# Layer normalisation scaled on another engine, and the first batch placed from SBUF to SBUF, in an attention and mixture-of-experts kernel

## The reference

```python
def _layernorm(x, axis=-1, eps=1e-05):
    m = jnp.mean(x, axis=axis, keepdims=True)
    v = jnp.var(x, axis=axis, keepdims=True)
    return (x - m) / jnp.sqrt(v + eps)

# attention: 16 heads of 16 channels, 256 queries, 512 keys (256 projected, 256 memory rows)
q = x1 @ Wq + bq;  k = concat(x2 @ Wk + bk, memory);  v = concat(x2 @ Wv + bv, memory)
out = softmax(q @ k.T * 0.25) @ v;  x = x + out @ Wp + bp
# experts: 8 of 256 -> 1024 -> 256, all of them applied to all tokens
g = x2 @ w_gate;  u = x2 @ w_up;  h = silu(g) * u;  expert_out = h @ w_down
cw = softmax(x2 @ w_router) * softmax(x2 @ w_gating / 0.1), normalised over the experts
x = x + sum_e cw[e] * expert_out[e]
```

## Time and profile before

| | |
|---|---|
| median of 3 runs | 2712.37 us (2711.29 to 2715.34) |
| profiled execution | 2711.55 us |
| its span, first to last instruction | 2709.8 us |
| PE busy | 2660.4 us (98%) |
| DVE busy | 2007.7 us (74%) |
| POOL busy | 1651.8 us (61%) |
| ACT busy | 1526.0 us (56%) |
| mean granted clock of TensorE | 0.991 of full speed |
| chain that ended last, by engine | PE 94%, DVE 4%, issue 1%, DMA 1% |

### The profile page before, as it was taken

The page is one execution under the profiler, slowest core; times in us unless marked ns, Lnnn a source line. Parts: engine busy times, 40 slices in busy tenths (PEclk is TensorE's granted clock), DMA queues, the critical chain, the costliest instruction groups (busy, mean ns, idle before and its releaser), DMA issues.

```text
span 2709.8 us, 46807 instructions
## 1 busy us (share of the span) xinstructions
PE 2660.4 (98%) x15969; PEld 2184.3 (81%) x15969; DVE 2007.7 (74%) x3303; ACT 1526.0 (56%) x2887; POOL 1651.8 (61%) x1837
## 2 busy tenths in 40 slices
PE   6899999999999999999999999999999999999998
PEld 5578888888888888888888888888888888888887
DVE  6987777777778777777777777777787777655554
ACT  4655555555555555555555555555555555544443
POOL 4766666666656666566666566666566666655554
PEclk8899999999999999999999999999999999999999
DMA  6344434444333443433434433444333442333332
GB/s 166 101 112 122 127 100 118 132 120 123 115 118 115 120 126 115 127 109 112 131 115 131 120 116 108 125 122 131 113 105 114 126 122 88 97 107 113 108 102 82
DMA packets 298427, 315.44 MB, mean 116 GB/s; under 512 B 22096, under 2 KB 269264, under 8 KB 298192
## 3 DMA queue, kind: packets, MB, share of 16 engines
q1 hardware_dynamic: 298192, 312.45, 39.0%
HBM read 278.15 MB, written 33.69 MB: 115 GB/s over the span
## 4 chain that ended last, share of the span: by engine, by line
PE 94%; DVE 4%; issue 1%; DMA 1%; POOL 0%; ACT 0%; SPq 0%; POOLq 0%; DVEq 0%; ACTq 0%
PE ps_s L706 26%; PE ps_t L706 26%; PE ps_o L740 25%; PE ps_s L803 4%; PE ps_t L813 4%; PE ps_a L782 2%; PE ps_a L784 2%; PE ps_m L586 1%; PE ps_m L615 1%; DVE negmax L1187 1%; PE ps_m L604 1%; DVE Pt_lo L1059 1%; PE ps_m L659 0%; DMA d_k<-kT_lo 0%; PE ps_m L677 0%
## 5 line engine op out<-in xcount | busy, mean ns | idle before, releaser
L969 DVE SCALAR_TENSOR_TENSOR hf<-hf,ps_s 128x512 f32<-128x512 f32 x512 | 350.2, 684 | 326.7 <-ACT hf L827 324.8
L833 ACT ACTIVATE h_hi<-ps_t 128x512 fp32r<-128x512 f32 x512 | 306.1, 598 | 440.2 <-DVE ps_t L976 440.2
L1221 POOL TENSOR_TENSOR wg_lo<-stage_w,wg_hi 128x512 fp32r<-128x512 f32 x256 | 330.9, 1292 | 339.5 <-ACT wg_hi L840 337.9
L827 ACT ACTIVATE hf<-ps_s 128x512 f32<-128x512 f32 x512 | 306.4, 598 | 410.5 <-PE ps_s L706 410.5
L981 DVE TENSOR_TENSOR h_lo<-ps_t,h_hi 128x512 fp32r<-128x512 f32 x512 | 353.0, 689 | 211.9 <-ACT h_hi L833 205.6
L740 PE MATMUL ps_o<-h_lo,wd_hi 128*128 128x512 f32 x1024 | 400.1, 391 | 0.0
L740 PE MATMUL ps_o<-h_hi,wd_hi 128*128 128x512 f32 x1024 | 398.5, 389 | 0.9 <-DVE h_lo L981 0.9
L740 PE MATMUL ps_o<-h_hi,wd_lo 128*128 128x512 f32 x1024 | 398.4, 389 | 0.0
L976 DVE TENSOR_TENSOR ps_t<-hf,ps_t 128x512 f32<-128x512 f32 x512 | 356.4, 696 | 52.9 <-PE ps_t L706 6.2
L1221 POOL TENSOR_TENSOR wd_lo<-stage_w,wd_hi 128x512 fp32r<-128x512 f32 x256 | 330.8, 1292 | 93.0 <-ACT wd_hi L840 93.0
L947 ACT ACTIVATE Pt<-ps_t 128x512 f32<-128x512 f32 x512 | 305.8, 598 | 142.1 <-PE ps_t L813 134.1
(11 more groups left out here) (208 smaller groups left out, 4734.3 us busy)
## 6 DMA issues: line engine op xcount, KB each, us to landing
stage_w<-in_L_ffn_w_gate_dram SPq DMA_DIRECT2D x256, 256.0 KB, 2.8
stage_w<-in_L_ffn_w_up_dram SPq DMA_DIRECT2D x256, 256.0 KB, 3.1
stage_w<-in_L_ffn_w_down_dram SPq DMA_DIRECT2D x256, 256.0 KB, 2.8
KTs<-d_k SPq DMA_DIRECT2D x96, 256.0 KB, 4.9
cwb<-d_cw SPq DMA_DIRECT2D x64, 256.0 KB, 3.6
QTs<-d_q SPq DMA_DIRECT2D x192, 64.0 KB, 2.7
X<-in_x_dram SPq DMA_DIRECT2D x32, 256.0 KB, 4.5
d_k<-kT_hi SPq DMA_DIRECT2D x16, 512.0 KB, 4.1
```

The source lines that it names most:

```text
L827: act.activation(hf[:], ps_g[:], ACT.Tanh, scale=0.5).then_inc(tanh_done, 1)
L833: act.activation(h_hi[f % FC][:], ps_u[:], ACT.Copy).then_inc(hh_done, 1)
L969: dve.scalar_tensor_tensor(out=hf[:], in0=hf[:], scalar=1.0, in1=ps_g[:], op0=ALU.add, op1=ALU.mult).then_inc(gate_done, 1)
L1221: pool.tensor_tensor(lo[:], raw_weights(n), hi[:].bitcast(F32), ALU.subtract).then_inc(wl_done, 1)
```

## The change

1. **Statistics.** One `bn_aggr` for each of the two token tiles gives mean and variance, and two `tensor_scalar` of 128x2 add epsilon and negate the mean. They are ready one step earlier than before.
2. **Applying them.** GpSimd multiplies the negated mean by the scale into `shift` (one more instruction of 128x2). ScalarE computes scale * x + shift, at step 13 (`X1`) and step 28 (`X`, formerly 29 on VectorE).
3. **First batch.** `place_first` at step 10 of turn -1 copies each pair from `kT` and `qT` directly to `KTs` and `QTs`, 9 transfers for each of 8 pairs (3 of 64 KB, 6 of 16 KB), 72 in a row on SP. Batch 0 is not stored to DRAM and not read back. PE waits pair by pair; whoever overwrites `kT` or `qT` for batch 1 waits for all 72.
4. **First loads.** The three `stage_w` loads move to steps 20 to 22 of turn 0. `key_rows` has 3 rows instead of 32 (48 KB), the GpSimd memset of all of it is gone, and the key product reads 99 partitions.
5. **First q.** "q" of turn -1 gets its own PSUM bank, `ps_t[1]`.

```diff
@@ norm_stats
-                    dve.tensor_tensor(m[:, :, 2:4], stt[:, :, 1:3], stt[:, :, 4:6], ALU.add).then_inc(mv_c.sem, 1)
-                    dve.tensor_tensor(m[:, :, 1], stt[:, :, 1], stt[:, :, 4], ALU.subtract).then_inc(mv_c.sem, 1)
+                    for t in range(QT):
+                        dve.bn_aggr(m[:, t, 0:2], stt[:, t, :]).then_inc(mv_c.sem, 1)
                 if step == at + 2:
-                    turn.wait(dve, mv_c, d, 2)
-                    dve.tensor_scalar(m[:, :, 0], m[:, :, 2], 0.5, None, ALU.mult).then_inc(mv_c.sem, 1)
-                    dve.tensor_scalar(m[:, :, 4], m[:, :, 3], 1.0 / D, LN_EPS, ALU.mult, ALU.add).then_inc(mv_c.sem, 1)
-                    dve.scalar_tensor_tensor(out=m[:, :, 5], in0=m[:, :, 1], scalar=0.25, in1=m[:, :, 1],
-                                             op0=ALU.mult, op1=ALU.mult).then_inc(mv_c.sem, 1)
-                if step == at + 3:
-                    turn.wait(dve, mv_c, d, 5)
-                    dve.tensor_tensor(v[:], m[:, :, 4], m[:, :, 5], ALU.add).then_inc(ve_c.sem, 1)
+                    turn.wait(dve, mv_c, d, QT)
+                    dve.tensor_scalar(v[:], m[:, :, 1], LN_EPS, None, ALU.add).then_inc(ve_c.sem, 1)
+                    dve.tensor_scalar(m[:, :, 2], m[:, :, 0], -1.0, None, ALU.mult).then_inc(ve_c.sem, 1)
@@ GpSimd, step 26 (and the same at step 12 for X1)
                         pool.tensor_tensor(rstd[:], ve[:], neg_half[:], ALU.pow).then_inc(rstd_done.sem, 1)
+                        turn.wait(pool, rstd_done, 2, 1)
+                        pool.tensor_tensor(shift[:], mv[:, :, 2], rstd[:], ALU.mult).then_inc(shift_done.sem, 1)
@@ ScalarE (VectorE's normalise, called at steps 13 and 29, is gone)
+            def normalise(src, r, s, dst, done):
+                for t in range(QT):
+                    act.activation(dst[:, t, :], src[:, t, :], ACT.Identity, bias=s[:, t:t + 1],
+                                   scale=r[:, t:t + 1]).then_inc(done.sem, 1)
@@ SP
+            def place_first():
+                eng.wait_ge(k_l.sem, 2)
+                eng.wait_ge(m_l.sem, 1)
+                for pair in range(PAIRS):
+                    m, at = pair // GP, pair % GP * ROWS
+                    for slot, part in enumerate((kT_hi, kT_lo, kT_hi)):
+                        eng.dma_start(KTs[slot * ROWS:(slot + 1) * ROWS, pair, :].bitcast(F32),
+                                      part[at:at + ROWS, m, :].bitcast(F32)).then_inc(first_in[pair], 16)
+                    if pair == 0:
+                        eng.wait_ge(q_l.sem, 2)
+                        eng.wait_ge(const_ready, CONSTS)
+                    for slot, part in enumerate((qT_hi, qT_hi, qT_lo)):
+                        for h in range(2):
+                            to, row = slot * ROWS + h * HD, at + h * HD
+                            eng.dma_start(QTs[to:to + HD, pair, h, :].bitcast(F32),
+                                          part[row:row + HD, m, :].bitcast(F32)).then_inc(first_in[pair], 16)
@@ SP, the order of the steps
-                    if turn.has(1) and step == (10 if first else 14):
-                        store_keys(turn, 1)
...
+                    if turn.b == -1 and step == 10:
+                        place_first()
+                    if turn.b == 0 and step >= 20 and step - 20 < 3:
+                        load_weights(step - 20, 0)
@@ TensorE
+                        if turn.b + d == 0:
+                            if i % 4 == 0:
+                                pe.wait_ge(first_in[i // 4], 16 * 9)
...
-                        pe.matmul(key_bank(j)[:], KTs[:, pair, kc * P:(kc + 1) * P],
-                                  QTs[:, pair].rearrange("p h n -> p (h n)"),
+                        pe.matmul(key_bank(j)[:], KTs[0:USED, pair, kc * P:(kc + 1) * P],
+                                  QTs[0:USED, pair].rearrange("p h n -> p (h n)"),
@@ bank
-            return ps_m[:] if one else ps_o[:, 1, :]
+            return ps_t[1][:] if one is None else ps_m[:] if one else ps_o[:, 1, :]
```

More of the change, by code:

```diff
@@ L53, in bass_xattn_moe_ffn_kernel @@
     TOP = 3 * ROWS
+    USED = TOP + 3
     GP = PAIRS // 2
@@ L224, in bass_xattn_moe_ffn_kernel @@
         v_ps = Count("v_ps", 1); v_done = Count("v_done", 1)
+        first_in = [sem(f"first_in{p}") for p in range(PAIRS)]
         k_in = [Count(f"k_in{g}", 16 * 3) for g in range(2)]
@@ L245, in bass_xattn_moe_ffn_kernel, with wait_stored @@
         cwT_ps = Count("cwT_ps", 1); cwT_done = Count("cwT_done", 1)
-        CONSTS = 7
+        CONSTS = 6
         LAST = (START + FSTEPS) // STEPS
+        def wait_stored(eng, turn, count):
+            if turn.b == 0:
+                for arrived in first_in:
+                    eng.wait_ge(arrived, 16 * 9)
+            else:
+                turn.wait(eng, count, -1, 32)
         class Turn:
@@ L808, in body @@
                         pair, kc = i // KC, i % KC
+                        if turn.b == 0 and i == 0:
+                            pe.wait_ge(rows_in, 16)
                         if kc == 0:
@@ L881, in body @@
                         split_high(n)
+                    if step == 13 and turn.has(-1):
+                        turn.wait(act, shift2_done, -1, 1)
+                        turn.wait(act, x2T_ps, -2, 1)
+                        normalise(X1, rstd2, shift2, X2, x2_done)
+                    if step == 28 and turn.has(2):
+                        turn.wait(act, shift_done, 2, 1)
+                        turn.wait(act, xT_ps, 1, 1)
+                        normalise(X, rstd, shift, XN, xn_done)
                     for o, at, d in v_at(turn):
@@ L922, in body @@
                         turn.wait(act, full, 1, 1)
-                        turn.wait(act, used, 0, 32)
+                        wait_stored(act, turn, used)
                         for m in range(DC):
@@ L1060, in low_part @@
                                       ALU.subtract).then_inc(lo_dve.sem, 1)
-            def normalise(turn, d, src, m, r, dst, done):
-                for t in range(QT):
-                    dve.tensor_scalar(dst[:, t, :], src[:, t, :], m[:, t, 0:1], r[:, t:t + 1],
-                                      ALU.subtract, ALU.mult).then_inc(done.sem, 1)
             def body(turn):
@@ L1162, in body @@
                                           ALU.add).then_inc(x1_done.sem, 1)
-                    if step == 13 and turn.has(-1):
-                        turn.wait(dve, rstd2_done, -1, 1)
-                        turn.wait(dve, x2T_ps, -2, 1)
-                        normalise(turn, -1, X1, mv2, rstd2, X2, x2_done)
                     if name == "lg":
@@ L1177, in body @@
                                           ALU.subtract).then_inc(ldif_done.sem, 1)
-                    if step == 29 and turn.has(2):
-                        turn.wait(dve, rstd_done, 2, 1)
-                        turn.wait(dve, xT_ps, 1, 1)
-                        normalise(turn, 2, X, mv, rstd, XN, xn_done)
                     d, i = item_at(step, AHEAD)
@@ L1204, in _ @@
             pool.memset(zeros[:], 0.0).then_inc(const_ready, 1)
-            pool.memset(key_rows[:], 0.0).then_inc(rows_clear, 1)
             pool.memset(QTs[:].bitcast(F32), 0.0).then_inc(const_ready, 1)
```

85 lines of the change are left out of this document (44 added, 41 removed).

## The result

| | before | after |
|---|---|---|
| median | 2711.14 us (6 runs) | 2731.14 us (6 runs, 2728.82 to 2731.73) |
| ratio after / before, 95% interval | | 1.0070 (1.0057 to 1.0083) |
| profiled execution, its span | 2711.55, 2709.8 us | 2728.82, 2726.8 us |

The account below looks back on a forecast made before the run. PE was taken to bound the joint stage and VectorE the attention stage, with the opening ahead. From 2712.4 us, 3.2 us for the opening and 4.3 us for the normalisations gave -7.5 us: 2704.9 us, 8-in-10 range 2697 to 2712 us.

Parts of the forecast that it names:

- What bounds the kernel: Joint stage: PE always busy, so no gain there; attention stage: VectorE bound; the end moves as the experts' start does.
- The opening, up to the first score: Batch 0's first placing: SP issues at 14.5 us, first score at 21.1 us, 10.5 us sooner; 3.2 us finally kept.
- 72 issues ... 0.46 us each ... ends at 47.7 us: SP's queue in the opening: all placing transfers issue ahead of turn 0's work, bounds 0.43 to 0.51 us each.
- what is late next: Turn 0, step 12: VF load behind the 72 issues stalls PE's "m" 7 us, leaving 3.4 of 10.5 us.
- The normalisations: Four layer normalisations before the experts: net 6.5 us off VectorE, two thirds, 4.3 us, reaching the end; bounds 1 to 7.
- The stronger form with GpSimd's share given back: Attention stage: VectorE and GpSimd both regain time lost to their shared port lock, making the 4.3 us about 6.
- Slow copies: Rival, 8%: SBUF-to-SBUF data take 47 us, last pair lands at 62 us, VF behind it; about 2716 us.
- Fast placing: Rival, 12%: small transfers issue at 0.35 us, VF is not late, opening keeps 10 us; 2698 us.
- The gain stays in the opening: Rival, 29%: issues cost 0.51 us or VectorE's relief becomes waits for ScalarE; one part lost, 2707 to 2712 us.
- Edits at no cost: 99-partition key product, late stage_w loads and ScalarE's 0.84 us in the joint stage were claimed to cost nothing.

Follow-up runs that it names:

- own_tiles: Changed kernel with batch 0's keys and queries in tiles free until turn 1, the 72 transfers kept; 2726.37 us, ratio 1.0045.
- own_tiles_vf: own_tiles with the VF load issued ahead of the last 18 of the 72 transfers; 2719.18 us, ratio 1.0018.
- pair0_direct: Kernel before with parts 1, 2, 4 and 5, first of eight pairs copied SBUF to SBUF, seven by DRAM; 2705.49 us, ratio 0.9970.
- dram_source: Changed kernel with batch 0 stored to DRAM first and the same 72 transfers reading it there; 2724.19 us, one run.
- place_only: Changed kernel with the layer normalisations of the kernel before, parts 3, 4 and 5 left; 2732.82 us, ratio 1.0072.
- stats_only: Kernel before with bn_aggr and one small addition for the statistics, VectorE still applying mean and scale; 2710.82 us, ratio 0.9988.
- loads_only: Kernel before with parts 4 and 5 alone, batch 0 still by DRAM; 2711.94 us, ratio 0.9996.
- pair0_warm3: pair0_direct with three extra identity transposes on PE ahead of each small job of turns 0 and 1; ratio 0.9975.

## Why the prediction was wrong

Starts of steps on PE (the key product, from the timelines, us) beside what each kernel ends with. The steps and the spans are of one profiled execution each, the last row is of all runs:

| | before | after | own_tiles | own_tiles_vf | pair0_direct |
|---|---|---|---|---|---|
| turn 0, step 0 | 39.7 | 34.5 | 34.0 | 34.1 | 33.2 |
| turn 0, step 6 | 48.5 | 65.9 | 44.1 | 42.6 | 43.4 |
| turn 0, step 12 | 55.5 | 73.6 | 68.2 | 54.5 | 50.8 |
| turn 0, step 24 | 71.3 | 90.0 | 85.2 | 78.7 | 66.4 |
| turn 2, step 14 | 157.2 | 174.6 | 170.5 | 163.0 | 151.1 |
| span of that execution | 2709.8 | 2726.8 | 2724.7 | 2715.2 | 2705.8 |
| end, by the ratio | | +19.0 | +12.2 | +4.9 | -8.1 |

**What bounds the kernel.** Right. The joint stage gave nothing for VectorE's 64 us, and the end moved by about as much as the steps just ahead of the experts: step 14 of turn 2 is 17.4 us late in the changed kernel and its span 17.0 us longer.

**The opening, up to the first score.** The chain to SP's first issue was right within 0.1 us. The first score came at 22.53 us, 1.4 us later than forecast. The nine issues of the first pair ended at 21.28 us instead of 18.8. The six of `QTs` took 0.9 us more, and they began 1.6 us late: the third issue of the burst alone took 1.80 us, 1.2 us more than its neighbours (why is open), and the rest is the dearer issue. PE then began 1.25 us later, where 2.3 us had been taken. Step 0 of turn 0, which needs the third pair, started at 34.5 us instead of 29.4 us, because the pairs come every 5.7 us.

**The step that failed first: "72 issues ... 0.46 us each ... ends at 47.7 us".** The price came from placings whose source is DRAM, with bounds of 0.43 and 0.51 us from the same rows. For a copy from SBUF to SBUF it is 0.633 us, outside both; dram_source shows that the source makes the difference. 72 x (0.633 - 0.46) = 12.5 us, and the burst ended 13.7 us later than forecast; most of the rest is the one issue of 1.80 us. The rows were of another kind, and no upper bound was drawn for that. The prediction read the only SBUF-to-SBUF transfer in the trace as a rate of data and not for its issue, which took 0.75 us; 72 of those would be 54 us, past every case that it considered.

**The step that was left out: "what is late next".** It looked along SP's queue alone and found `VF` at step 12, which own_tiles confirms as the second wait. The first is at step 4: whoever overwrites `kT` waits for all 72. The change's own list said so, and the sum had no term for it. This omission decides even at the forecast's price: burst ended at 47.7 us, plus the 1.35 us measured from last issue to ScalarE, is 49.05 us, against 45.70 us in the kernel before. The 3.2 us gain of the opening becomes a loss of 3.4 us, and with 4.3 us for the normalisations the whole comes to about no change. The dearer issue then makes it 17.1 us late. dram_source confirms this reading near its own price: "k" 11.0 us late, the end 10.5 us late.

**From 17.1 to 19 us.** The profiled execution of the changed kernel is the fastest of its six. Its span is 17.0 us longer than that of the kernel before, as much as "k" is late; the other five are 1.7 to 2.9 us slower, and for those there is no trace. The changed kernel is also as slow as place_only (1.0070 and 1.0072), so the 3 us of the normalisations do not show in it. The intervals, each about 3.5 us to a side, leave this open.

**The normalisations.** 4.3 us forecast, 3.0 us measured, within the interval. `bn_aggr` took 0.156 us (0.1 taken), the first `tensor_scalar` 0.227 us instead of 0.63, ScalarE's instruction 0.59 us instead of 0.42. The size came out, but the argument for it, that VectorE is relieved by 10 us and so the end by two thirds of the net, is not borne out: stats_only leaves VectorE its two large instructions and gains as much. What ScalarE adds (two of 0.59 us for each normalisation, and 2.7 and 3.0 us of waiting for `shift` at the two `X1`) is a price on an engine between PE and VectorE. The stronger form with GpSimd's share given back, 6 us, lies outside the interval.

**The rivals.** *Slow copies* was the side on which it fell, at 8%, and by the wrong resource. It decided from 0.57 us per transfer on, and 0.633 us is past that. But it spoke of the time of the data, and it reached the loss by way of `VF`: in the changed kernel PE started "m" at 72.93 us without a wait for `VF`, since "k" had made everything later. In the DMA view of the changed kernel, 14 to 62 us, 16 engines are busy for a fifth and each transfer lands in 2 us:

```profile
DMA packets 2658, 2.37 MB, mean 49 GB/s; under 512 B 1136, under 2 KB 1888, under 8 KB 2656
...
q1 hardware_dynamic: 2656, 2.35, 19.9%
...
KTs<-kT_hi SPq DMA_DIRECT2D x16, 64.0 KB, 2.0
...
QTs<-qT_hi SPq DMA_DIRECT2D x32, 16.0 KB, 1.8
```

The engines had room; the queue that issues was full. The Trainium skill, "DMA: Bandwidth & Descriptors", section "Bandwidth", has it that transfers under 64 KB are dominated by descriptors. This trace is no test of that: its 49 GB/s follow from the time between two issues on SP. The same page of the Trainium skill, section "Anatomy of one DMA — SWDGE (gpsimd) path", speaks of another path, and calls the cost of generating descriptors small and variable. What part of an issue on SP that is, no run here shows; the whole issue was 0.45 or 0.63 us for every transfer, times 72. *Fast placing* asked for 0.35 us an issue: no run shows it. *The gain stays in the opening* describes loads_only, not the change.

**Edits at no cost.** The 99 partitions: right, nothing shows. The late `stage_w`, the thin `key_rows` and the own bank for q: together, without the placing, they bring the first score 4.1 us forward (loads_only), which the prediction had credited to the placing alone.

## What to carry to other kernels

Here the copy that replaced a round trip was paid at the issuing queue. So count its transfers, price an issue from one with both ends in the same memories, even if the trace has only one, and list everybody who stands behind the last of them, on the queue itself and through each tile that the transfers still read. In this kernel 9 direct transfers for the pair that is wanted first gained about 4 us (8 us together with the other parts of the change), and 72 lost 19. When one wait is mended, look for the next behind the same queue before running the kernel: there were three, at steps 4, 12 and 24, and each mended one left the next.

## What the runs showed of the hardware

- From one issue on SP to the next it took 0.45 us for loads from DRAM to SBUF (dram_source) and 0.633 us for copies from SBUF to SBUF (changed kernel), with no visible difference between 16 and 64 KB. Issues of stores from SBUF to DRAM took 0.36 to 0.52 us in the opening of the kernel before. One issue early in the burst took 1.80 us.
- Transfers from SBUF to SBUF of 16 and 64 KB landed in 1.8 and 2.0 us in the median, with the DMA engines busy for a fifth.
- `bn_aggr` from 6 to 2 values on 128 partitions took 0.156 us; ScalarE's activation of 128x256 with scale and bias per partition took 0.59 us, a plain copy of that size 0.42 us. The output was f32 in the one and bf16 in the other, which these runs do not separate.
- With the mean granted clock raised from 0.86 to 0.95 between 55 and 200 us by extra products (pair0_warm3 against pair0_direct), in a stage where PE hands over to other engines at every step, the ratio went from 0.9970 to 0.9975, each within 0.001: no change that could be measured.
